# Attention and feed-forward block on one core: O transposed into SBUF and normalised one batch at a time

## The chip, the cores and the metric

The kernel runs on one core of one Trainium2 chip. The metric is the device time of one execution in microseconds. Engines are named as in the profile: PE (TensorE), PEld (its weight loads), DVE (VectorE), ACT (ScalarE), POOL (GpSimd), SP (SyncE, which issues all DMAs here).

## The reference, cut to what matters

For 16 batches of 256 tokens with 256 features in float32 (Python, shortened):

```
xn  = layernorm(x)                              # x: (16, 256, 256)
q, k, v = split(xn @ w_qkv)                     # 16 heads of 16
scores  = where(causal, (q / 4) @ k.T, -1e10)
o   = softmax(scores) @ v                       # per batch and head
out = x + o @ w_out + ffn(xn)                   # ffn: gated GELU in fp8, 256 -> 1024 -> 256
```

The output is (16, 256, 256) in float32.

## The kernel before, in words

The first third (to about 110 us) does the layernorm and the feed-forward part, adds its result to `xres` in SBUF, and stores the transposed, normalised tokens split into two fp32r parts. The rest is attention, one batch per step: the loop `for s in range(B)` in each engine's block (lines 1024, 564, 741, 374, 279), with B = 16. All order is written out by hand, an engine at a time; engines meet only at semaphores, and each engine takes its instructions strictly in order.

A batch b passes through several steps:

- `project_qk` and `project_v` (L845, L852, PE) make q, k and v; ACT copies and rounds them (L636, L642), POOL takes the low part (`split_qk`, L337), SP copies both parts into `stack` (`fill_stack`, three DMAs, L251).
- `max_scores(b, n)` for six units n = 0..5 (L905, PE) writes scores into three rotating banks of PSUM, and DVE's `find_max(b, n)` (L531) masks them and takes row maxima. `max_scores` of unit n waits (`max_done`, L898) until DVE has finished the first half of unit n - 1.
- `transpose_max(b, c)` (L963, PE) turns the maxima of half the heads (c = 0 or 1) once all their units are found; ACT negates them (L656), SP puts them into `stack` (`place_max`, L256).
- `exp_scores(b, n)` (L932, PE) waits for that DMA at n = 0 and 3, and for ACT's previous `exponent` (L663), since all units share two banks. ACT exponentiates into `arena`, POOL zeroes the masked half of diagonal blocks (`mask`, L366).
- `times_v(b, c)` (L954, PE, 32 passes) makes O for half the heads in one bank of PSUM (`pv_bank`), transposed and with the denominators as extra rows. Its next use of this bank waits for `o_norm_done` (L946).
- DVE: `o_to_rows(b, c)` (L540) transposes that bank in place in 32x32 blocks; `normalize_o(b, c)` takes the reciprocal of the denominators (L546), multiplies (L548, inputs: the bank in PSUM and `r_den` in SBUF; output `o_norm`), and transposes 128x256 into `ot_raw` (L555). ACT rounds it (`round_ot`, L672), POOL takes the low part (`split_ot`, L371), PE multiplies by w_out (`project_out`, L975), DVE adds `xres` (`add_x`, L561), SP stores it (L266).

In step s, PE works on maxima of batch s, exponentials of s - 1, O of s - 2 and s - 1, and the output of s - 3. In the order of time PE runs: `exp_scores(s-1, 0)`, `max_scores(s, 0)`, `transpose_max(s-1, 1)`, ..., `max_scores(s, 5)`, `times_v(s-1, 0)`. DVE runs `find_max(s-1, 5)`, `o_to_rows(s-2, 0)`, `find_max(s, 0..1)`, `normalize_o(s-2, 0)`, `find_max(s, 2)`, `o_to_rows(s-2, 1)`, `find_max(s, 3..4)`, `normalize_o(s-2, 1)`, `add_x(s-3)`. What comes after the loop (lines 1080 to 1101 of PE) ends the last two batches; `keep_warm(n, bank)` (L797) issues n transposes whose result nobody reads.

On SP, `fill_stack(s+1, 0)`, `load_xs(s+3)`, `store_y(s-4)` and `place_max(s, 0)` stand in this order in one queue. In the feed-forward part POOL waits for DVE's last normalisation of a chunk before it starts (line 343).

Of the kernel before, what the change touches and what calls it, by code (L numbers as in the profile page):

```python
# [31 lines left out]
def attention_ffn(nc, x, w_qkv, w_out, w_gating, w_linear, out):  # L32
# [25 lines left out]
    with ctx:  # L58
# [45 lines left out]
        r_den = sb("r_den", [P, H], F32)  # L104
# [1 line left out]
        o_norm = sb("o_norm", [P, S], F32)
        ot_part = xt_part[:, :, :, 0:S]
# [191 lines left out]
        def _(pool):  # L299
# [73 lines left out]

            for s in range(B):
                if has(s - 2):
                    mask(s - 2, 5)
                if has(s - 3):
                    split_ot(s - 3, 1)
# [10 lines left out]
                if has(s - 2):  # L389
                    split_ot(s - 2, 0)  # L390
# [13 lines left out]
        def _(dve):  # L404
# [136 lines left out]

            def normalize_o(b, c):
                done = 2 * b + c + 1
                o = pv_bank(b, c).rearrange("p (k e) -> p k e", e=2 * DH)
# [10 lines left out]
                nc.vector.transpose(ot_raw[:, c, :], o_norm[:, :]).then_inc(ot_ready, 1)  # L555

            def add_x(b):
# [3 lines left out]
                nc.vector.tensor_tensor(y[b % 2][:, :, :], misc[:, 0, :].rearrange("p (t d) -> p t d", t=QT),  # L561
                                        xres[:, b * QT:(b + 1) * QT, :], ALU.add).then_inc(y_done, 1)

            for s in range(B):
# [563 lines left out]
```

## Time and profile before

| | |
|---|---|
| median of 3 runs | 353.01 us (353.0 to 353.84) |
| profiled execution | 353.47 us, of it the span 351.8 us |
| busy over the span | PE 336.5 us (96%), DVE 294.5 (84%), ACT 227.2 (65%), POOL 167.8 (48%) |
| chain that ended last | PE 81%, DVE 10%, ACT 3%, issue 2%, DMA 2% |
| granted TensorE clock, mean | 0.995 |

The span runs from the first to the last instruction of the profiled execution, and all positions below are microseconds from its start. A group row gives busy time, then in brackets what the engine waited for before it. Matmul ends are modelled, so the start of the next PE group is the safer mark of when one was over. A step of attention takes 14.3 us: `exp_scores(s-1, 0)` starts at 291.17, 305.47 and 319.14 for s = 13, 14 and 15.

### The profile page before, as it was taken

Reading aid. Unit: us, or ns where it says so; the run is one execution under the profiler, and the core shown is the slowest. Engines: PE = TensorE matmul, PEld = TensorE weight load, DVE = VectorE, ACT = ScalarE, POOL = GpSimd, SP = SyncE. Lnnn points to the kernel's source line nnn. Section 1 sums busy time; section 2 is a strip of 40 time slices with the busy share of each in tenths; the row PEclk is TensorE's granted clock in tenths of the full one; section 3 lists DMA queues with packets and bytes.
Section 4 is the critical chain, followed back from the end, with each engine's and each line's share of the span. In section 5 each row is a group of like instructions: output and inputs, shape, how many; then the busy total and the mean of one; then the engine's idle time right before and its main releaser. Section 6 shows DMA issues by size and latency. Waiting matters only on the chain.

```text
span 351.8 us, 9794 instructions
## 1 busy us (share of the span) xinstructions
PE 336.5 (96%) x3514; PEld 256.8 (73%) x3514; DVE 294.5 (84%) x1359; ACT 227.2 (65%) x369; POOL 167.8 (48%) x203
## 2 busy tenths in 40 slices
PE   6899899999999999999999999999999999996996
PEld 6455456665676878788888888888888888884775
DVE  5897898888425787999999999899999999999865
ACT  1684777766655576676667766767667666775470
POOL 4214214422225364456675466664755657547461
PEclk9999999999999999999999999999999999999899
DMA  6959965673238243534528346274373552633011
GB/s 204 366 191 294 269 177 154 144 244 123 74 137 295 96 151 108 199 114 161 181 94 270 113 162 209 101 237 165 111 241 108 196 183 92 212 120 127 2 64 60
DMA packets 46569, 57.59 MB, mean 164 GB/s; under 512 B 2680, under 2 KB 39096, under 8 KB 46520
## 3 DMA queue, kind: packets, MB, share of 16 engines
q1 hardware_dynamic: 46520, 56.96, 49.9%
q8 instruction: 28, 0.46, 0.5%
q14 instruction: 21, 0.17, 0.2%
HBM read 16.78 MB, written 12.58 MB: 83 GB/s over the span
## 4 chain that ended last, share of the span: by engine, by line
PE 81%; DVE 10%; ACT 3%; issue 2%; DMA 2%; POOL 0%; SPq 0%; DVEq 0%; ACTq 0%; POOLq 0%
PE ps L954 13%; PE ps L845 13%; PE ps L932 11%; PE ps L905 9%; PE ps L852 7%; PE ps L832 7%; PE ps L975 6%; PE ps L809 6%; PE ps L815 6%; DVE masked L531 4%; PE ps L963 2%; PE ps L792 2%; ACT gate L618 1%; DMA xt_store<-stack 1%; DVE xn L432 1%
## 5 line engine op out<-in xcount | busy, mean ns | idle before, releaser
L531 DVE CUSTOM_DVE_ANT_0 masked<-ps,causal 128x256 bf16<-128x256 f32 (+1 forms) x512 | 148.2, 353 | 17.1 <-PE ps L905 17.1
L663 ACT ACTIVATE arena<-ps 128x1024 f32<-128x1024 f32 x96 | 98.1, 1026 | 54.7 <-PE ps L932 54.4
L366 POOL TENSOR_SCALAR_AFFINE_SELECT arena<-arena 128x512 f32<-128x512 f32 (+1 forms) x96 | 73.6, 787 | 32.9 <-ACT arena L663 32.9
L337 POOL TENSOR_TENSOR qk_part<-w_raw,qk_part 128x512 fp32r<-128x512 f32 x32 | 41.2, 1286 | 52.1 <-ACT qk_part L642 52.1
L618 ACT ACTIVATE gate<-ps 128x512 bf16<-128x512 f32 x64 | 38.6, 603 | 28.6 <-PE ps L809 28.3
L932 PE MATMUL ps<-stack 64*128 64x256 f32 (+1 forms) x512 | 51.4, 300 | 2.3 <-ACT arena L663 2.2
L845 PE MATMUL ps<-xs,wq_part 128*128 128x256 f32 x384 | 52.3, 285 | 0.3 <-ACT w_raw L636 0.3
L954 PE MATMUL ps<-arena,v_aug 128*32 128x256 f32 (+1 forms) x1024 | 49.5, 335 | 1.8 <-DVE o_norm L548 1.8
L905 PE MATMUL ps<-stack 63*128 63x256 f32 (+1 forms) x512 | 47.7, 285 | 2.0 <-DVE row_max L531 1.8
L845 PEld LDWEIGHTS ps<-xs,wq_part 128*128 128x128 f32 x384 | 47.5, 189 | 1.5 <-ACT w_raw L636 0.6
L932 PEld LDWEIGHTS ps<-stack 64*128 64x128 f32 x512 | 36.0, 186 | 15.0 <-issue 5.7
L531 DVE DVE_READ_ACCUMULATOR2_ANT row_max<- 128x1 f32 x512 | 42.6, 83 | 0.0
L954 PEld LDWEIGHTS ps<-arena,v_aug 128*32 128x32 f32 x1024 | 29.7, 111 | 17.4 <-issue 3.5
L905 PEld LDWEIGHTS ps<-stack 63*128 63x128 f32 x512 | 36.4, 187 | 6.4 <-DVE row_max L531 3.3
L333 POOL TENSOR_TENSOR xres<-xres,ffn 128x512 f32<-128x512 f32 x16 | 18.3, 1157 | 38.4 <-DVE xn L432 28.0
L468 DVE TENSOR_TENSOR arena<-ps,gate 128x512 fp8e4<-128x512 f32 x32 | 22.0, 687 | 15.7 <-ACT gate L618 15.3
L371 POOL TENSOR_TENSOR xt_part<-xn,xt_part 128x256 fp32r<-128x256 f32 x31 | 22.7, 731 | 20.0 <-ACT xt_part L672 20.0
L975 PE MATMUL ps<-wq_part,xt_part 128*128 128x256 f32 x192 | 30.7, 296 | 0.1
L540 DVE STREAM_TRANSPOSE ps<-ps 128x512 f32<-128x512 f32 x32 | 23.4, 731 | 5.3 <-PE ps L954 5.3
L468 DVE TENSOR_TENSOR act<-ps,gate 128x512 fp8e4<-128x512 f32 x32 | 21.8, 685 | 6.3 <-ACT gate L618 6.3
L852 PE MATMUL ps<-wq_part,xs 128*128 128x256 f32 x192 | 26.7, 288 | 0.0
L975 PEld LDWEIGHTS ps<-wq_part,xt_part 128*128 128x128 f32 x192 | 24.7, 189 | 2.8 <-issue 0.4
(64 smaller groups left out, 454.0 us busy)
## 6 DMA issues: line engine op xcount, KB each, us to landing
stack<-qk_part SPq DMA_DIRECT2D x96, 256.0 KB, 2.7
xs<-xt_store SPq DMA_DIRECT2D x16, 512.0 KB, 4.2
xt_store<-xt_part SPq DMA_DIRECT2D x14, 512.0 KB, 4.2
out_dram<-w_raw SPq DMA_DIRECT2D x15, 256.0 KB, 4.2
xres<-in_L_attn_x_dram SPq DMA_DIRECT2D x7, 512.0 KB, 6.6
arena<-in_L_ffn_w_gating_dram SPq DMA_DIRECT2D x2, 1024.0 KB, 9.3
stack<-zeros SPq DMA_DIRECT2D x4, 512.0 KB, 7.8
arena<-in_L_ffn_w_linear_dram SPq DMA_DIRECT2D x1, 1024.0 KB, 13.3
```

The lines of the kernel that those rows point to most:

```text
L337: nc.gpsimd.tensor_tensor(qk_part[:, g, QLO:KLO + 1:3, :], qk_raw[:, g, :, :], qk_part[:, g, QHI:KLO, :].bitcast(F32), ALU.subtract).then_ ...
L366: nc.gpsimd.affine_select(diag, diag, pattern=[[0, 1024 // width], [1, P]], compare_op=ALU.is_ge, fill=0.0, base=0, channel_multiplier=-1) ...
L468: nc.vector.tensor_tensor(act8[c % 2][:, j, :], up_ps[j % 2], gate[:, j % 2, :], ALU.mult, saturate=False).then_inc(act_done, 1)
L531: last = nc.vector.tensor_tensor_reduce(masked[:, place, i * width:(i + 1) * width], max_ps[:, place, i * width:(i + 1) * width], causal[: ...
L618: nc.scalar.activation(gate[:, j % 2, :], gate_ps[j % 2], ACT.Gelu_apprx_tanh).then_inc(gelu_done, 1)
L663: nc.scalar.activation(arena[:, n, :, :], exp_banks(b, n), ACT.Exp).then_inc(exp_done, 1)
L845: last = nc.tensor.matmul(misc[:, 1, s * S:(s + 1) * S], wq_part[:, a, kt, col:col + P], xs[b % 2][:, z, kt, :], start=(i == 0), stop=(i = ...
L852: last = nc.tensor.matmul(misc[:, 0, t * D:(t + 1) * D], xs[b % 2][:, z, kt, t * P:(t + 1) * P], wq_part[:, a, kt, 2 * D:3 * D], start=(i ...
L905: last = nc.tensor.matmul(max_ps[:, (2 * unit + u) % 3, i * width:(i + 1) * width], st[rows, j0 + i, 0, qt * P:(qt + 1) * P], st[rows, j0 ...
L932: last = nc.tensor.matmul(exp_banks(b, n)[:, u, i * width:(i + 1) * width], st[rows, j0 + i, 1, kt * P:(kt + 1) * P], st[rows, j0 + i, 0, ...
L954: last = nc.tensor.matmul(pv_bank(b, c)[32 * i:32 * i + 32, u * S + kt * P:(u + 1) * S], va[:, kt, 2 * (HG * c + i) + u, :], cols, start=( ...
L975: last = nc.tensor.matmul(y_bank(b, t), ot_part[:, z, c, t * P:(t + 1) * P], wq_part[:, a, c, 3 * D:4 * D], start=(first and i == 0), stop ...
```

## The change

1. `o_to_rows` transposes from PSUM into a new place `o_by_q[b % 2]` in SBUF (it reuses `wg8` and `act8[0]`, dead by then). `times_v` waits for `o_by_q_done` in place of `o_norm_done`.
2. `normalize_o` is called once a batch, on 32 denominators and 128x512 values, all of them in SBUF, for every batch but the last (`by_batch`). It stands where `normalize_o(s-2, 1)` stood. Likewise `round_ot` (ACT) and `split_ot` (POOL) are called once, 128x512, in the place of their former c = 1 calls. `ot_part` exists twice.
3. In step 15 and after it: DVE does `find_max(15, 5)` and `o_to_rows(14, 0)` before the normalisation of batch 13; `project_out(12, 1)` moves behind `times_v(14, 1)`; `project_out(13, 0)` behind `times_v(15, 0)`; `project_out(13, 1)` and both of batch 14 behind `times_v(15, 1)`; `keep_warm` is 8 in one place where it was 4 and 12 in two. Batch 14 gets the other bank of `misc` for its output.

The diff, without the bodies that only change an index:

```diff
             def o_to_rows(b, c):
 
                 dve.wait_ge(pv_ready, 2 * b + c + 1)
-                nc.vector.transpose(pv_bank(b, c), pv_bank(b, c)).then_inc(o_by_q_done, 1)
+                if b >= 2:
+
+                    dve.wait_ge(o_norm_done, 2 * b - 2)
+                nc.vector.transpose(o_by_q[b % 2][:, :, c, :], pv_bank(b, c).rearrange("p (u n) -> p u n", u=2)).then_inc(o_by_q_done, 1)
...
+                n = 2 if by_batch(b) else 1
+                half = slice(c, c + n)
+                done = 2 * b + c + n
+                o = o_by_q[b % 2][:, :, half, :].rearrange("p u c (k e) -> p u (c k) e", e=2 * DH)
+                den = r_den[:, :, half, :].rearrange("p u c k -> p u (c k)")
                 dve.wait_ge(o_by_q_done, done)
-                nc.vector.reciprocal(r_den[:, :], o[:, :, DH]).then_inc(den_done, 1)
+                nc.vector.reciprocal(den, o[:, :, :, DH]).then_inc(den_done, n)
...
+                nc.vector.tensor_tensor(o_norm[:, half, :].rearrange("p c (k u d) -> p u (c k) d", u=2, d=DH), o[:, :, :, 0:DH],
+                                        den.unsqueeze(3).broadcast_to([P, 2, n * S // 32, DH]), ALU.mult).then_inc(o_norm_done, n)
...
-                nc.scalar.copy(ot_part[:, 0, c, :], ot_raw[:, c, :]).then_inc(ot_hi, 1)
+                    act.wait_ge(ot_used, 2 * b + c + n - 4)
+                nc.scalar.copy(ot_part[b % 2][:, 0, half, :], ot_raw[:, half, :]).then_inc(ot_hi, n)
...
                 elif 2 * b + c >= 1:
-                    pe.wait_ge(o_norm_done, 2 * b + c)
+                    pe.wait_ge(o_by_q_done, 2 * b + c)
...
             exp_scores(B - 1, 0)
-            pe.wait_ge(y_done, B - 3)
-            project_out(B - 3, 0)
             pe.wait_ge(neg_done[0], B)
             transpose_max(B - 1, 1)
-            project_out(B - 3, 1)
             exp_scores(B - 1, 1)
             exp_scores(B - 1, 2)
             times_v(B - 2, 1)
+            project_out(B - 4, 1)
             for n in range(3, UNITS):
                 exp_scores(B - 1, n)
             times_v(B - 1, 0)
-            pe.wait_ge(y_done, B - 2)
-            project_out(B - 2, 0)
-
-            keep_warm(4, misc[:, 1, :])
+            pe.wait_ge(y_done, B - 3)
+            project_out(B - 3, 0)
             times_v(B - 1, 1)
-            project_out(B - 2, 1)
+            project_out(B - 3, 1)
+
+            pe.wait_ge(neg_done[1], B)
+            for c in range(2):
+                project_out(B - 2, c)
             pe.wait_ge(exp_done, UNITS * B)
             project_out(B - 1, 0)
-            keep_warm(12, misc[:, 1, :])
+            keep_warm(8, max_ps[:, 0, :])
             project_out(B - 1, 1)
```

On DVE, the end of step 14 before: after `find_max(14, 4)` the second half of batch 12 is normalised, then batch 11 gets `add_x`, then the maxima of unit 5 follow.

```order
L531 ISA masked,row_max<-ps,causal 128x256
L531 ISA row_max 128x1
L546 RECIPROCAL r_den<-ps 128x16 [waits o_by_q_done]
L548 TENSOR_TENSOR o_norm<-ps,r_den 128x2x8x16 [waits den_done]
L555 STREAM_TRANSPOSE xn<-o_norm 128x256 [waits ot_lo,o_norm_done]
L561 TENSOR_TENSOR w_raw<-ps,xres 128x512 [waits y_stored1,ot_used]
L531 ISA masked,row_max<-ps,causal 128x256 [waits max_ready]
```

The same place after the change:

```order
L537 ISA masked,row_max<-ps,causal 128x256
L537 ISA row_max 128x1
L559 RECIPROCAL r_den<-wg 128x32 [waits o_by_q_done]
L561 TENSOR_TENSOR xn<-wg,r_den 128x2x16x16 [waits den_done]
L566 STREAM_TRANSPOSE xn<-xn 128x512 [waits ot_lo,o_norm_done]
L573 TENSOR_TENSOR w_raw<-ps,xres 128x512 [waits y_stored1,ot_used]
L537 ISA masked,row_max<-ps,causal 128x256 [waits max_ready]
```

The three instructions of the normalisation became twice as long here, and the three in front of `find_max(s, 2)` are gone. The product reads `wg` (O) and `r_den`, both in SBUF, where it read `ps` and `r_den`.

On PE, the end before, from `times_v(15, 0)`'s last passes (L954) on:

```order
L954 MATMUL ps<-arena,v_aug 32x128 x4
L975 MATMUL ps<-wq_part,xt_part 128x256 [waits ot_lo,y_done]
L975 MATMUL ps<-wq_part,xt_part 128x256 x5
L797 MATMUL ps<-ident 128x128 x4
L954 MATMUL ps<-arena,v_aug 32x256 [waits o_norm_done,p_masked1]
```

and from `times_v(15, 1)`'s last passes on:

```order
L954 MATMUL ps<-arena,v_aug 32x128 x4
L975 MATMUL ps<-wq_part,xt_part 128x256 [waits ot_lo]
L975 MATMUL ps<-wq_part,xt_part 128x256 x5
L975 MATMUL ps<-wq_part,xt_part 128x256 [waits ot_lo,exp_done]
L975 MATMUL ps<-wq_part,xt_part 128x256 x5
L797 MATMUL ps<-ident 128x128 x12
L975 MATMUL ps<-wq_part,xt_part 128x256 [waits ot_lo_last]
L975 MATMUL ps<-wq_part,xt_part 128x256 x5
```

After the change, from `times_v(15, 1)`'s last passes on:

```order
L965 MATMUL ps<-arena,v_aug 32x128 x4
L986 MATMUL ps<-wq_part,xt_part 128x256 [waits ot_lo]
L986 MATMUL ps<-wq_part,xt_part 128x256 x5
L986 MATMUL ps<-wq_part,xt_part 128x256 [waits ot_lo,neg_done1]
L986 MATMUL ps<-wq_part,xt_part 128x256 x5
L986 MATMUL ps<-wq_part,xt_part 128x256 [waits ot_lo]
L986 MATMUL ps<-wq_part,xt_part 128x256 x5
L986 MATMUL ps<-wq_part,xt_part 128x256 [waits ot_lo,exp_done]
L986 MATMUL ps<-wq_part,xt_part 128x256 x5
L808 MATMUL ps<-ident 128x128 x8
L986 MATMUL ps<-wq_part,xt_part 128x256 [waits ot_lo_last]
L986 MATMUL ps<-wq_part,xt_part 128x256 x5
```

Behind the last `times_v` stand four groups of `project_out` ahead of the last one, where two stood, and eight transposes where twelve stood.

On POOL, the start of a step before: `mask(s-2, 5)`, `split_ot(s-3, 1)`, `split_qk(s+1, 0)`.

```order
L366 AFFINE_SELECT arena<-arena 128x4x128 [waits exp_done]
L371 TENSOR_TENSOR xt_part<-xn,xt_part 128x256 [waits ot_hi]
L337 TENSOR_TENSOR qk_part<-w_raw,qk_part 128x2x256 [waits qk_hi0]
```

and after:

```order
L373 AFFINE_SELECT arena<-arena 128x4x128 [waits exp_done]
L380 TENSOR_TENSOR xt_part<-xn,xt_part 128x2x256 [waits ot_hi]
L344 TENSOR_TENSOR qk_part<-w_raw,qk_part 128x2x256 [waits qk_hi0]
```

`split_ot` is twice as wide in this place and gone from its other one, behind `mask(s-1, 4)`.

## Rows read from the trace of the kernel before

**Rows 1.** Stretches: us, busy (count) by engine, clock, DMA share, GB/s.

```profile
280.00:300.00 20.00, 20.00 (x262) 16.64 (x259) 18.40 (x98) 14.17 (x22) 11.94 (x15) 1.00 0.40 134
```

**Rows 2.** Timeline of PE, start of step 14: start us, us, instruction group.

```profile
305.97 0.61 PE L905 MATMUL ps<-stack 63*128 63x128 f32 x8
306.51 0.38 PE L963 MATMUL ps<-ident,row_max 128*8 128x128 f32 x2
```

**Rows 3.** Timeline of ACT, POOL and DVE, end of step 13.

```profile
301.84 0.61 ACT L642 CAST qk_part<-w_raw 128x512 fp32r<-128x512 f32 x1
...
302.54 1.30 POOL L337 TENSOR_TENSOR qk_part<-w_raw,qk_part 128x512 fp32r<-128x512 f32 x1 [3.27 <-ACT qk_part L642]
...
302.54 0.25 DVE L546 RECIPROCAL r_den<-ps 128x16 f32<-128x16 f32 x1
302.83 0.42 DVE L548 TENSOR_TENSOR o_norm<-ps,r_den 128x256 f32<-128x256 f32 x1
303.29 0.45 DVE L555 STREAM_TRANSPOSE xn<-o_norm 128x256 f32<-128x256 f32 x1
...
303.66 0.65 DVE L561 TENSOR_TENSOR w_raw<-ps,xres 128x512 f32<-128x512 f32 x1
...
304.23 0.41 DVE L531 CUSTOM_DVE_ANT_0 masked<-ps,causal 128x256 bf16<-128x256 f32 x1
...
305.61 0.73 DVE L540 STREAM_TRANSPOSE ps<-ps 128x512 f32<-128x512 f32 x1
```

**Rows 4.** All L323 of POOL (ns min/median/max), and timeline at 13.8 us.

```profile
L323 POOL TENSOR_TENSOR rstd<-var_eps,minus_half x8: 1036/1037/1601, 5.9 to 80.7; 128x4 f32<-128x4 f32 x8
...
13.79 1.60 POOL L323 TENSOR_TENSOR rstd<-var_eps,minus_half 128x4 f32<-128x4 f32 x1
13.81 0.69 DVE L479 CAST wg<-arena 128x1024 fp8e4<-128x1024 f32 x1
```

**Rows 5.** Timeline of ACT, POOL and SP's queue, step 13.

```profile
295.63 0.40 ACT L672 CAST xt_part<-xn 128x256 fp32r<-128x256 f32 x1
...
296.11 0.73 POOL L371 TENSOR_TENSOR xt_part<-xn,xt_part 128x256 fp32r<-128x256 f32 x1 [1.47 <-ACT xt_part L672]
...
296.80 1.29 POOL L337 TENSOR_TENSOR qk_part<-w_raw,qk_part 128x512 fp32r<-128x512 f32 x1
...
298.12 1.87 SPq L251 DMA_DIRECT2D stack<-qk_part  x3
```

**Rows 6.** Timeline of PEld and SP's queue, starts of steps 5 and 8.

```profile
176.72 0.52 PEld L932 LDWEIGHTS ps<-stack 64*128 64x128 f32 x8 [0.23 <-DMA stack<-neg_max]
219.63 0.52 PEld L932 LDWEIGHTS ps<-stack 64*128 64x128 f32 x8 [0.20 <-DMA stack<-neg_max]
...
172.40 0.57 SPq L256 DMA_DIRECT2D stack<-neg_max  x1
...
216.19 0.57 SPq L256 DMA_DIRECT2D stack<-neg_max  x1
```

**Rows 7.** Timeline of PE from the end of step 14 on.

```profile
317.70 1.51 PE L954 MATMUL ps<-arena,v_aug 128*32 128x256 f32 x32 [0.65 <-DVE o_norm L548]
...
321.51 0.50 PE L905 MATMUL ps<-stack 63*128 63x256 f32 x4 [0.95 <-DVE row_max L531]
...
324.45 2.79 PE L954 MATMUL ps<-arena,v_aug 128*32 128x256 f32 x32 [0.35 <-DVE o_norm L548]
...
332.43 1.51 PE L954 MATMUL ps<-arena,v_aug 128*32 128x256 f32 x32 [0.65 <-DVE o_norm L548]
...
344.84 1.69 PE L975 MATMUL ps<-wq_part,xt_part 128*128 128x256 f32 x12
...
346.37 1.47 PE L797 MATMUL ps<-ident 128*128 128x128 f32 x12
...
347.90 0.97 PE L975 MATMUL ps<-wq_part,xt_part 128*128 128x256 f32 x6
```

**Rows 8.** The stretch of the lower clock, columns as in rows 1.

```profile
324.40:327.80 3.40, 3.35 (x40) 2.19 (x42) 2.25 (x10) 0.54 (x1) 1.24 (x3) 0.54 0.00 0
```

More of the change, by code:

```diff
@@ L103, in attention_ffn @@
         y = [w_raw[:, 0, i * QT * D:(i + 1) * QT * D].rearrange("p (t d) -> p t d", t=QT) for i in range(2)]
[L104 removed]
+        r_den = sb("r_den", [P, 2, 2, S // 32], F32)
+        o_by_q = [t.bitcast(F32).rearrange("p (u c n) -> p u c n", u=2, c=2)
+                  for t in (wg8[:, :, :, :].rearrange("p g k n -> p (g k n)"), act8[0][:, :, :].rearrange("p j t -> p (j t)"))]
         ot_raw = xn[:, 2:4, :]
[L106 to L107 removed]
+        o_norm = xn[:, 0:2, :]
+        ot_part = [xt_part[:, :, :, i * S:(i + 1) * S] for i in range(2)]
         ps = ctx.enter_context(nc.psum_tensor("ps", [P, 8, 512], F32))
@@ L161, in y_bank, with by_batch @@
         def y_bank(b, t):
-            return exp_ps[:, t, 0:D] if b == B - 1 else misc[:, 0, t * D:(t + 1) * D]
+            return exp_ps[:, t, 0:D] if b == B - 1 else misc[:, int(b == B - 2), t * D:(t + 1) * D]
+        def by_batch(b):
+            return b < B - 1
         block = ctx.enter_context(nc.Block())
@@ L377, in _ @@
                 if has(s - 3):
-                    split_ot(s - 3, 1)
+                    split_ot(s - 3, 0)
                 if s >= 1 and has(s + 1):
@@ L554, in normalize_o @@
                     dve.wait_ge(ot_lo, done - 2)
-                nc.vector.transpose(ot_raw[:, c, :], o_norm[:, :]).then_inc(ot_ready, 1)
+                nc.vector.transpose(ot_raw[:, half, :].rearrange("p c s -> p (c s)"),
+                                    o_norm[:, half, :].rearrange("p c s -> p (c s)")).then_inc(ot_ready, n)
             def add_x(b):
@@ L580, in _ @@
                     find_max(s, 4)
+                if s == B - 1:
+                    find_max(s, 5)
+                    o_to_rows(s - 1, 0)
                 if has(s - 2):
-                    normalize_o(s - 2, 1)
-                if has(s - 3):
+                    normalize_o(s - 2, 0)
+                if has(s - 3) and s < B - 1:
                     add_x(s - 3)
-            find_max(B - 1, 5)
-            o_to_rows(B - 2, 0)
+            o_to_rows(B - 2, 1)
+            add_x(B - 4)
             normalize_o(B - 2, 0)
-            add_x(B - 3)
-            o_to_rows(B - 2, 1)
-            normalize_o(B - 2, 1)
             for c in range(2):
@@ L745, in _ @@
                 if has(s - 3):
-                    round_ot(s - 3, 1)
+                    round_ot(s - 3, 0)
                 if has(s + 1):
@@ L756, in _ @@
                     negate_max(s, 0)
-                if has(s - 2):
-                    round_ot(s - 2, 0)
                 if has(s - 1):
@@ L770, in _ @@
                     round_qk(s + 2, 0)
-            round_ot(B - 3, 1)
             exponent(B - 1, 0)
@@ L776, in _ @@
             exponent(B - 1, 2)
-            round_ot(B - 2, 0)
+            round_ot(B - 3, 0)
             for n in range(3, UNITS):
                 exponent(B - 1, n)
-            round_ot(B - 2, 1)
+            round_ot(B - 2, 0)
             for c in range(2):
@@ L942, in times_v @@
                 if b == B - 1:
-                    pe.wait_ge(*((max_done, 2 * UNITS * B) if c == 0 else (o_norm_done, 2 * b)))
+                    pe.wait_ge(*((max_done, 2 * UNITS * B) if c == 0 else (o_by_q_done, 2 * b)))
                 elif 2 * b + c >= 1:
-                    pe.wait_ge(o_norm_done, 2 * b + c)
+                    pe.wait_ge(o_by_q_done, 2 * b + c)
                 for u in range(2):
@@ L1065, in _ @@
                     max_scores(s, 4)
-                if has(s - 3):
+                if has(s - 3) and s < B - 1:
                     project_out(s - 3, 1)
```

39 lines of the change are left out of this document (16 added, 23 removed).

## The prediction

> **What bounds the kernel now.** I read the stretches first. From 160 to 300 us PE has no idle time at all: 20.00 of 20 us, with DVE at 18.40, ACT at 14.17 and POOL at 11.94 [rows 1]. A step there takes as long as its PE instructions, so an edit on DVE, ACT or POOL can't shorten it; it can only put a wait into PE's row. So the question for each of the twelve full steps is a margin: how long before PE wanted it was each result ready. Then I read the timeline for the two places where a DVE result is nearly late. At the start of step 14 PE starts `max_scores(14, 0)` at 305.97, which needs the first half of `find_max(13, 5)`, and `transpose_max(13, 1)` at 306.51, which needs all of it [rows 2]. DVE starts that `find_max` at 304.23 and is through at 305.61, when its next instruction starts [rows 3]; half of it is then done at about 304.92. The margins are 1.05 and 0.90 us, less about 0.1 for the semaphore. Last I read the end, from step 14 on, where PE does wait: 0.65 us ahead of 317.70, 0.95 ahead of 321.51, 0.35 ahead of 324.45 and 0.65 ahead of 332.43; the three of `times_v` are for `o_norm_done` [rows 7]. One `times_v` there takes 2.79 us where the others take 1.51, and the clock granted between 324.4 and 327.8 is 0.54, so for most of it the lower level, 1.2 GHz [rows 7, 8]. The idle stretches come just ahead of it.
>
> **The waits for o_norm_done.** They go, since the bank is free after one transpose. In the full steps PE never waited there, so that is worth nothing. At the end it can be worth up to 0.65 + 0.35 + 0.65 = 1.65 us, if nothing else is late next.
>
> **The merged normalisation on DVE.** Per batch one set of three instructions goes and the other doubles. The product grows by 0.23 us (0.65 of a 128x512 TENSOR_TENSOR less 0.42 of the 128x256 one), the transpose by 0.28 (0.73 less 0.45), the reciprocal by some 0.02 [rows 3]. DVE gains in sum: a set took 302.54 to 303.66, 1.12 us, and the growth is 0.53, so 0.6 us a step less work. But the gain lies ahead of `find_max(s, 2)`, where DVE waits for PE anyway, and the growth lies ahead of `find_max(s, 5)`. That one moves from 304.23 to 304.76. Of the margins 1.05 and 0.90 remain 0.52 and 0.37, less 0.1. Price in the full steps: nothing, but the cover is then 0.3 us thin.
>
> **What the product now reads.** Before, L548 read O from PSUM and the denominators from SBUF. Now both inputs lie in SBUF. It would start at about 302.85, and POOL has been in `split_qk` since 302.54 and stays until 303.84 [rows 3]; POOL's start hangs on ACT's rounding (L642, 301.84), which follows PE, so the two meet like this in every full step. Does one of the two block the other? No row shows a DVE instruction with two SBUF inputs beside a POOL one. The nearest row: L323 on POOL takes 1.04 us in seven of eight places and 1.60 where it started within 0.02 us of a DVE copy from SBUF to SBUF (L479, 0.69 us). POOL lost 0.56 of 0.69 us, four fifths of what the other took; DVE lost nothing, the copy ran like its peers [rows 4]. So a blocking exists between these engines, and it is nearly whole. In the new place POOL is first by 0.3 us, so DVE should be the one that loses. Bounds: 0, and 0.98 us (302.85 to 303.84). I take four fifths of the upper one, 0.8 us, by rows 4. Then all maxima are found at 305.61 + 0.53 + 0.8 = 306.94, PE sees it at 307.04 and not at 306.51: 0.53 us in each step. By the upper bound it is 0.71. The step repeats rigidly from PE to PE, so the loss isn't made up: it comes at the start of steps 3 to 14, twelve times, 6.4 us (0 to 8.5).
>
> The Trainium skill's page "SBUF — State Buffer", section "Who interferes with whom", says that a DVE instruction with two SBUF inputs contends with a GpSimd instruction that reads SBUF, that whichever starts first holds the shared pair for its whole instruction, and that a DVE instruction with at most one SBUF input does not contend. By that the sum would take the upper end. The trace agrees as far as it goes: L548 and L555, one SBUF input each, keep their 0.42 and 0.45 us beside POOL's 1.30 [rows 3]; two inputs no run has shown yet.
>
> **POOL and ACT ahead of fill_stack.** ACT's `round_ot` grows from 0.40 to 0.61 us (L642 has the new width, rows 3), POOL's `split_ot` from 0.73 to 1.29 (as L337). POOL stands idle for `round_ot` here (1.47 us), and `split_qk(s+1, 0)` and SP's `fill_stack(s+1, 0)` follow without a gap [rows 5]. So this train of DMAs starts 0.21 + 0.56 = 0.77 us later, and behind it in SP's queue stand `load_xs`, `store_y` and `place_max(s, 0)`, which `exp_scores(s, 0)` waits for. The place of that DMA shows a thin margin: in step 5 it was issued at 172.40 and let PE go at 176.72, 4.3 us later; in step 8, issued late at 216.19, it did so at 219.63, 3.4 us later [rows 6]. With 3.4 us an ordinary issue has 0.9 us to spare and 0.77 costs nothing; with 4.3 it costs all of it. Two of the ten full steps name the DMA, so I take 2 x 0.77 = 1.5 us (0 to 8 x 0.77 = 6). If the product blocks as above, PE waits for DVE in the same half microsecond afterwards and a stall at `exp_scores` is largely contained in it, so then I count nothing more.
>
> **The end.** The first wait, 0.65 ahead of 317.70, goes, but `find_max(14, 5)` comes 0.53 later and with it everything of DVE up to the 0.95 us wait ahead of 321.51: PE gets there at 322.04, later than before. `times_v(13, 1)` loses its 0.35 and starts at about 324.6, 0.2 late. PE has idled as much before it, so I keep its 2.79 us. After that PE saves 0.65 at 332.43 and several groups of `project_out` move back; what binds is ACT's exponentials, and I get `times_v(15, 1)` ending 1.1 us earlier than 344.84. Behind it come four groups of six passes where two took 344.84 to 346.37, 0.77 each, and 8 transposes where 12 took 1.53 [rows 7]: + 1.53 - 0.51 = + 1.0. The remainder, rounding, low part and last product, is the same. Net 0.1 us gain or loss, taken as + 0.1 for the store of batch 13 that now falls near the end. A blocked product in step 14 adds its 0.8 at 321.51 once more, on a chain of DVE, PE and ACT that has no slack.
>
> **Sum.** 353.5 (profiled execution) + 6.4 + 0.8 + 0.1 = 360.8. The profiled execution is 0.46 above the median of 353.01, so against the medians 360.3 us.
>
> **Rivals.**
> 1. No blocking, but the DMA train is late: 353.0 + 1.5 + 0.1 = 354.6. For it: [rows 5, 6]; against it: eight of ten steps don't name the DMA. It decides where `place_max` lands less than 0.77 us before `exp_scores`.
> 2. Nothing new binds: 353.0 + 0.1 = 353.1. For it: DVE has less work, 0.3 us of cover is left. It needs both the product and the train to be hidden.
> 3. The other side, faster: no blocking, and PE keeps its full clock in step 15. The place is `times_v(13, 1)`: 1.51 in place of 2.79 us, 1.3 less, and the 0.2 it starts late is then swallowed by ACT. 353.1 - 1.4 = 351.7. For it: two waits of PE shortly before are removed or moved, and a clock that fell once beside 0.95 and 0.35 us waits may not fall with others. Against it: the wait for maxima ahead of 321.51 grows. It decides from the point where PE's idle time between 318 and 324 is less than before.
>
> The change surely does what it says on DVE; a variant of the forecast is a partial blocking, 0.3 to 0.5 us on the product, which costs 0.03 to 0.2 a step and ends between 353.5 and 356.
>
> **How the numbers follow.** A measurement of this kernel tells no change from one within about 0.3%, 1.06 us. Forecast (blocking) 0.47; rival 1 0.15; rival 2 0.16; rival 3 0.22. Faster by over 0.3% is rival 3, 0.22; within it rival 2 and a little of rival 1, 0.17; slower the rest, 0.61. The forecast's own range is 356 (partial) to 363.5 (the upper bound, 0.71 in twelve steps and 0.98 at the end: 353.0 + 8.5 + 1.0 + 0.1 = 362.6, and some for DMAs). The range for 8 in 10 must reach rival 3: 351.4 to 363.
>
> **What would show it.** The product (now L561) at about 1.2 to 1.6 us, or started that much late, where 0.65 is its free size; a period from `exp_scores` to `exp_scores` of 14.8 to 15.0 us where it was 14.3; PE waiting for `row_max` ahead of `transpose_max` in each step. If the product takes 0.65 to 0.70 beside `split_qk`, the forecast is wrong. If PE waits for `neg_max`'s DMA, it is rival 1; if no L954 is over 1.6 us long, rival 3.

## The result, and the profile after

| | before | changed kernel |
|---|---|---|
| median, taken together | 353.42 us (4 runs) | 368.49 us (366.15 to 369.75, 4 runs) |
| profiled execution, span | 353.47, 351.8 us | 368.86, 367.1 us |
| granted TensorE clock, mean | 0.995 | 0.981 |

The ratio is 1.0384 [1.0332, 1.0435], 15.1 us slower. The direction and the mechanism in the steps were as forecast; the size was twice the forecast's 7.3 us, and the time lies outside the range.

From the page of the changed kernel: busy time, the granted clock in 40 slices, and the chain that ended last. PE's share fell from 96% to 93% although it did 6 us more of busy time, and DVE's share of the chain rose from 10% to 23%.

```profile
PE 342.4 (93%) x3506; PEld 259.1 (71%) x3506; DVE 297.1 (81%) x1314; ACT 225.2 (61%) x354; POOL 171.7 (47%) x188
...
PEclk9999999999999999999999999999999999996599
...
PE 52%; DVE 23%; DMA 8%; issue 6%; ACT 4%; SPq 4%; POOL 2%; DVEq 0%; ACTq 0%; POOLq 0%
```

The timeline of DVE, POOL and PE where step 13 ends (start us, us, engine, line; what was waited for in brackets) answers to [rows 2, 3]:

```profile
296.56 0.35 DVE L559 RECIPROCAL r_den<-wg 128x32 f32<-128x32 f32 x1
296.56 1.29 POOL L344 TENSOR_TENSOR qk_part<-w_raw,qk_part 128x512 fp32r<-128x512 f32 x1 [2.44 <-ACT qk_part L654]
297.01 1.38 DVE L561 TENSOR_TENSOR xn<-wg,r_den 128x512 f32<-128x512 f32 x1
...
297.80 2.14 POOL L373 TENSOR_SCALAR_AFFINE_SELECT arena<-arena 128x1024 f32<-128x1024 f32 x2
...
298.49 0.71 DVE L566 STREAM_TRANSPOSE xn<-xn 128x512 f32<-128x512 f32 x1
...
299.12 0.65 DVE L573 TENSOR_TENSOR w_raw<-ps,xres 128x512 f32<-128x512 f32 x1
299.70 0.41 DVE L537 CUSTOM_DVE_ANT_0 masked<-ps,causal 128x256 bf16<-128x256 f32 x1
299.80 0.52 PEld L943 LDWEIGHTS ps<-stack 64*128 64x128 f32 x8 [0.50 <-DMA stack<-neg_max]
...
300.61 0.66 PE L916 MATMUL ps<-stack 63*128 63x128 f32 x8
...
301.07 0.71 DVE L549 STREAM_TRANSPOSE act<-ps 128x512 f32<-128x512 f32 x1
```

The product takes 1.38 us. Its record begins at 297.01, in the middle of POOL's `split_qk` (296.56 to 297.85), and ends at 298.39, 0.54 us behind POOL's end: a blocked instruction shows here as a long one, not as a late one. POOL loses as well: the two masks behind `split_qk`, which start beside the product, take 2.14 us, where the kernel without the overlap (e1 below) shows 1.68. From the reciprocal to `find_max(13, 5)` are 299.70 - 296.56 = 3.14 us, where it was 304.23 - 302.54 = 1.69 [rows 3].

All that PE and its loads waited for in the steps, 148 to 326 us (total us, times, longest):

```profile
PE ps L943 <- DMA stack<-neg_max: 2.7, 6, 1.3
PE ps L916 <- DVE row_max L537: 2.7, 8, 0.5
...
PEld ps L943 <- DMA stack<-neg_max: 5.3, 9, 1.6
```

Both suspects of the prediction show, DVE's maxima and the DMA behind the late train. A step that ran at 14.3 us takes 15.07, from one `transpose_max(s-1, 1)` on PE to the next:

```profile
301.30 0.38 PE L974 MATMUL ps<-ident,row_max 128*8 128x128 f32 x2
...
316.37 0.38 PE L974 MATMUL ps<-ident,row_max 128*8 128x128 f32 x2
```

The stretches of PE at the end (us, busy, granted clock, DMA share, GB/s), which answer to [rows 1, 8]:

```profile
300.00:320.00 20.00, 19.34 (x228) 1.00 0.35 121
...
330.00:340.00 10.00, 7.12 (x72) 0.68 0.23 79
340.00:350.00 10.00, 8.50 (x80) 0.64 0.00 1
...
333.60:347.30 13.70, 11.94 (x104) 0.50 0.06 20
```

The clock is at its lower level, 1.2 GHz, for 13.7 us, where it was 3.4 us before [rows 8]. PE's own timeline there answers to [rows 7]:

```profile
330.76 0.66 PE L916 MATMUL ps<-stack 63*128 63x128 f32 x8 [1.81 <-DVE row_max L537]
...
332.81 0.50 PE L916 MATMUL ps<-stack 63*128 63x256 f32 x4 [0.98 <-DVE row_max L537]
...
334.66 0.80 PE L943 MATMUL ps<-stack 64*128 64x256 f32 x4 [1.11 <-ACT arena L675]
...
335.82 2.79 PE L965 MATMUL ps<-arena,v_aug 128*32 128x256 f32 x32
...
345.30 2.46 PE L965 MATMUL ps<-arena,v_aug 128*32 128x256 f32 x32
```

Three waits of 1.81, 0.98 and 1.11 us stand around the fall. Before they were 0.95 and 0.35 [rows 7] and, between these two, 1.12, which this row of the kernel before shows:

```profile
323.37 0.50 PE L932 MATMUL ps<-stack 64*128 64x256 f32 x4 [1.12 <-ACT arena L663]
```

Two `times_v` are slow instead of one. Last, the kernel's final adds on DVE:

```profile
364.02 0.76 DVE L613 TENSOR_TENSOR w_raw<-ps,xres 128x256 f32<-128x256 f32 x2 [1.75 <-DMA out_dram<-w_raw]
```

The add waits 1.75 us, with the store of batch 13 named as releaser; before it waited 0.78 us for the last matmuls.

### The profile page after: what moved, and what is told of

The parts are those of the page before. It is cut to its first block, busy times and chain, and to the rows that moved or that the text cites. A ratio compares the mean times of both kernels' runs of the same rounds, so it can differ in the third digit from the quotient of the medians.

```text
span 367.1 us, 9748 instructions
## 1 busy us (share of the span) xinstructions
PE 342.4 (93%) x3506; PEld 259.1 (71%) x3506; DVE 297.1 (81%) x1314; ACT 225.2 (61%) x354; POOL 171.7 (47%) x188
## 4 chain that ended last, share of the span: by engine, by line
PE 52%; DVE 23%; DMA 8%; issue 6%; ACT 4%; SPq 4%; POOL 2%; DVEq 0%; ACTq 0%; POOLq 0%
DVE masked L537 10%; PE ps L856 8%; PE ps L916 8%; PE ps L965 6%; PE ps L943 6%; PE ps L863 6%; PE ps L843 5%; PE ps L820 5%; PE ps L826 5%; DVE xn L561 4%; DMA stack<-neg_max 3%; DMA xres<-in_L_attn_x_dram 2%; SPq L258 2%; PE ps L974 2%; DVE w_raw L573 1%
## 5 line engine op out<-in xcount | busy, mean ns | idle before, releaser
L373 POOL TENSOR_SCALAR_AFFINE_SELECT arena<-arena 128x512 f32<-128x512 f32 (+1 forms) x96 | 79.8, 852 | 41.2 <-ACT arena L675 41.1
L943 PE MATMUL ps<-stack 64*128 64x256 f32 (+1 forms) x512 | 52.5, 306 | 6.7 <-ACT arena L675 3.8
L916 PE MATMUL ps<-stack 63*128 63x256 f32 (+1 forms) x512 | 49.4, 292 | 6.7 <-DVE row_max L537 6.3
L943 PEld LDWEIGHTS ps<-stack 64*128 64x128 f32 x512 | 36.8, 191 | 20.4 <-ACT arena L675 5.5
L965 PE MATMUL ps<-arena,v_aug 128*32 128x256 f32 (+1 forms) x1024 | 50.5, 340 | 0.0
L916 PEld LDWEIGHTS ps<-stack 63*128 63x128 f32 x512 | 37.8, 192 | 12.5 <-issue 6.0
L380 POOL TENSOR_TENSOR xt_part<-xn,xt_part 128x512 fp32r<-128x512 f32 (+1 forms) x16 | 20.1, 1255 | 32.1 <-ACT xt_part L686 32.1
L863 PEld LDWEIGHTS ps<-wq_part,xs 128*128 128x128 f32 x192 | 23.5, 188 | 2.0
## 6 DMA issues: line engine op xcount, KB each, us to landing
arena<-in_L_ffn_w_linear_dram SPq DMA_DIRECT2D x1, 1024.0 KB, 13.7
```

Of the source, the lines that this page charges most:

```text
L373: nc.gpsimd.affine_select(diag, diag, pattern=[[0, 1024 // width], [1, P]], compare_op=ALU.is_ge, fill=0.0, base=0, channel_multiplier=-1) ...
L863: last = nc.tensor.matmul(misc[:, 0, t * D:(t + 1) * D], xs[b % 2][:, z, kt, t * P:(t + 1) * P], wq_part[:, a, kt, 2 * D:3 * D], start=(i ...
L916: last = nc.tensor.matmul(max_ps[:, (2 * unit + u) % 3, i * width:(i + 1) * width], st[rows, j0 + i, 0, qt * P:(qt + 1) * P], st[rows, j0 ...
L943: last = nc.tensor.matmul(exp_banks(b, n)[:, u, i * width:(i + 1) * width], st[rows, j0 + i, 1, kt * P:(kt + 1) * P], st[rows, j0 + i, 0, ...
L965: last = nc.tensor.matmul(pv_bank(b, c)[32 * i:32 * i + 32, u * S + kt * P:(u + 1) * S], va[:, kt, 2 * (HG * c + i) + u, :], cols, start=( ...
```

## The experiments

Each kernel's median is compared with that of the kernel before from the same chip. "Growth" is by how much `transpose_max(14, 0)` of the profiled execution came later than in the kernel before (313.65 us there), less the same for `transpose_max(2, 0)` (142.57 there): the loss of twelve steps alone. "Low clock" is the length of the stretch at 1.2 GHz ahead of PE's last products, again in the profiled execution. "Product" is the duration of the multiplication in `normalize_o` (us); where two are given, they are the first and the second half of a batch.

| kernel | product | growth | low clock | median, us | ratio [95%] |
|---|---|---|---|---|---|
| before | 0.42 | 0 | 3.4 | 353.4 to 353.6 | 1 |
| changed kernel | 1.38 | 9.6 | 13.7 | 368.49 | 1.0384 [1.0332, 1.0435] |
| e1_guard | 0.69 | 5.7 | 6.8 | 359.89 | 1.0168 [1.0118, 1.0218] |
| e2_swap | 1.38 | 9.0 | 6.8 | 366.78 | 1.0371 [1.0303, 1.0438] |
| e3_both | 0.69 | 1.1 | 13.7 | 359.94 | 1.014 [1.0064, 1.0215] |
| e4_halves | 0.98, 1.27 | 2.2 | 6.8 | 359.79 | 1.0169 [1.0115, 1.0223] |
| e5_sbuf_old_end | 0.98, 1.27 | 1.7 | 3.4 | 356.62 | 1.0099 [1.0065, 1.0132] |
| e6_guard_old_end | 0.42 | -0.3 | 6.8 | 354.44 | 1.0029 [1.0001, 1.0057] |
| e7_before_warm | 0.42 | 0.0 | none | 352.44 | 0.9968 [0.995, 0.9986] |
| e8_guard_warm | 0.42 | -0.3 | none | 351.80 | 0.9946 [0.9921, 0.9972] |
| e9_after_warm | 1.38 | 9.6 | none | 363.18 | 1.0273 [1.0243, 1.0304] |
| e10_both_warm | 0.69 | 1.0 | none | 353.88 | 1.0015 [0.9995, 1.0035] |
| e11_both_warm_y3 | 0.69 | 1.0 | none | 353.45 | 1.0007 [0.9985, 1.0029] |

**e1_guard: POOL waits until the product is done.** This adds nothing to DVE; it moves `split_qk(s+1, 1)` behind the product, so that the two never overlap.

```diff
 if s >= 1 and has(s + 1):
+    if has(s - 2):
+        pool.wait_ge(o_norm_done, 2 * (s - 2) + 2)
     split_qk(s + 1, 1)
```

> The changed kernel, but in each step from 2 on POOL's split_qk(s+1, 1) waits until DVE has finished the product of batch s-2, so that the two never run together. Theory 1 (the product with two SBUF inputs is blocked by POOL, and this is what makes PE late): the product takes 0.65 to 0.70 us where it took 1.38, find_max(s, 5) starts 0.7 us earlier, PE no longer waits for row_max in the full steps. Theory 2 (the DMA train behind fill_stack is late as well, by the wider split_ot): PE still waits for the neg_max DMA at the start of most steps. If theory 1 alone holds the time is 358 to 360 us (368.5 less twelve times 0.76). If the train binds by itself, 362 to 366. Rival (the product is slow by its own access pattern, not by POOL): it stays at 1.38 and the time at 368 or more.

Measured: 359.89 us. The product (L563 here; min/median/max in ns) is at its free size, and the masks of POOL behind it are short again:

```profile
L563 DVE TENSOR_TENSOR xn<-act,r_den x6: 692/693/693, 160.4 to 308.9; 128x512 f32<-128x512 f32 x6
...
295.99 1.68 POOL L373 TENSOR_SCALAR_AFFINE_SELECT arena<-arena 128x1024 f32<-128x1024 f32 x2
...
PE ps L945 <- DMA stack<-neg_max: 4.6, 6, 1.4
PEld ps L945 <- DMA stack<-neg_max: 7.1, 9, 1.7
```

The last two rows are all of the waits for other engines that the view lists for PE and its loads from 148 to 312 us. So with the blocking gone PE shows no wait for DVE, and of the 5.7 us of growth that remain, 4.6 are PE's six waits for the DMA behind the late train; e3_both shows what the other 1.1 are. The time lies where blocking alone was expected (358 to 360), and yet the train binds as well: that expectation priced a blocked product and nothing beside it.

**e2_swap: the train early again.** On POOL, `split_qk(s+1, 0)`, which the train waits for, goes ahead of the now longer `split_ot`.

```diff
-if has(s - 3):
-    split_ot(s - 3, 0)
 if s >= 1 and has(s + 1):
     split_qk(s + 1, 0)
+if has(s - 3):
+    split_ot(s - 3, 0)
```

> The changed kernel, but in each step POOL does split_qk(s+1, 0) ahead of split_ot(s-3), so that the three DMAs of fill_stack, and place_max behind them in the queue, start earlier than in the kernel before. Theory 1 (the blocked product alone sets the loss): PE waits for no neg_max DMA any more, but as long for row_max, and the time stays at 366 to 369 us. Theory 2 (the late DMA train sets it): the time falls to 359 to 362.

Measured: 366.78 us. The product stays at 1.38, and in the same stretch the only wait of PE is

```profile
PE ps L916 <- DVE row_max L537: 5.0, 11, 0.5
```

Eleven times, once a step. With the train early the growth is still 9.0 us, nearly that of the whole change. The two causes overlap, they don't add: 5.7 and 9.0 us with one of them, 9.6 with both, and 1.1 of each of these is what e3_both has with neither.

**e3_both: both edits.**

> Both edits at once: POOL's split_qk(s+1, 1) waits for the product, and split_qk(s+1, 0) goes ahead of split_ot(s-3). By both theories nothing else in the full steps is late: a step takes 14.3 us again, PE idles nowhere from 160 to 300 us, and the time is 357 to 359.5 us: what is then left above the kernel before, 4 to 6 us, is the end (lower clock for 13.7 us, four groups of project_out behind the last times_v, the last store). If the step stays above 14.5 us, a third cause is at work.

Measured: 359.94 us (355.79 to 360.26). The view lists no wait of PE for another engine between 148 and 312 us, and the growth is 1.1: blocked product and late train are all of the loss in the steps but this 1.1. The timeline shows what it is:

```profile
304.27 0.35 DVE L561 RECIPROCAL r_den<-act 128x32 f32<-128x32 f32 x1
...
306.72 0.41 DVE L539 CUSTOM_DVE_ANT_0 masked<-ps,causal 128x256 bf16<-128x256 f32 x1
...
307.71 0.61 PE L918 MATMUL ps<-stack 63*128 63x128 f32 x8
308.09 0.71 DVE L551 STREAM_TRANSPOSE wg<-ps 128x512 f32<-128x512 f32 x1
308.32 0.38 PE L976 MATMUL ps<-ident,row_max 128*8 128x128 f32 x2
```

From the reciprocal to `find_max(13, 5)` are 306.72 - 304.27 = 2.45 us, 0.76 more than the 1.69 before, with nothing blocked. The maxima are found at 308.09 and PE goes on 0.23 us later, as in the changed kernel (301.07 and 301.30); it is 0.22 to 0.24 us at this place in every full step of this kernel, where it was 0.87 us or more before. So of the 0.90 us of margin [rows 2, 3] only 0.67 can be used, and 0.76 - 0.67 = 0.09 us a step are lost, in waits too short for the view. Twelve times that is the 1.1. The merged normalisation costs this by its own length.

A step takes 14.4 us, as expected, and the time is 0.4 above its range (357 to 359.5). It is still 6 us slower than before, and now nearly all of that comes after 320 us. Its stretches (columns as above) show the clock:

```profile
320.00:330.00 10.00, 6.74 (x80) 0.77 0.31 107
330.00:340.00 10.00, 9.31 (x82) 0.55 0.00 1
```

**e4_halves: the changed kernel with its end, normalised half a batch at a time.** `by_batch` returns False, and the calls of `normalize_o`, `round_ot` and `split_ot` stand in the loop's old places. O stays in SBUF.

```diff
 def by_batch(b):
-    return b < B - 1
+    return False
```

> The changed kernel with O in SBUF as there, but normalised, rounded and split by halves, each half in the place where the kernel before had it; the order of the end is the changed one. It separates the two SBUF inputs from the merging. Theory 1: the half product ahead of find_max(s, 5) meets split_qk as well and takes 0.42 + 0.8 = 1.2 us; of the 0.90 us margin some 0.7 are usable, so 0.2 us a step are lost, 2.4 us in all, and no DMA is late; with the 5 us of the end 360 to 362 us. Rival (the merging itself costs, blocking is minor): the same 358 to 360. Rival (two SBUF inputs are slow in any form): every half product takes over 0.8 us, those too that no POOL instruction meets.

Measured: 359.79 us. The half products are blocked too. The first row has all of those that read one of the two buffers (min/median/max in ns: the first of a batch takes 0.98 us, the second 1.27), the others show a second one and POOL beside it:

```profile
L564 DVE TENSOR_TENSOR xn<-act,r_den x12: 982/1122/1275, 153.3 to 305.2; 128x256 f32<-128x256 f32 x12
...
290.41 1.28 POOL L344 TENSOR_TENSOR qk_part<-w_raw,qk_part 128x512 fp32r<-128x512 f32 x1 [3.09 <-ACT qk_part L660]
...
290.71 1.26 DVE L564 TENSOR_TENSOR xn<-wg,r_den 128x256 f32<-128x256 f32 x1
```

The product ends at 291.97, 0.28 us after POOL's 291.69. The first half product meets POOL's `split_ot`, and `split_qk` behind that takes 1.47 us instead of 1.28:

```profile
283.98 0.73 POOL L380 TENSOR_TENSOR xt_part<-xn,xt_part 128x256 fp32r<-128x256 f32 x1 [1.63 <-ACT xt_part L692]
284.01 0.99 DVE L564 TENSOR_TENSOR xn<-wg,r_den 128x256 f32<-128x256 f32 x1
```

It ends at 285.00, 0.29 us behind POOL's 284.71. Behind step 15, where no POOL instruction meets it, a half product takes 0.42 us (349.06 to 349.48), so two inputs in SBUF aren't slow by themselves. A growth of 2.2 us follows, 0.18 a step: with halves, some 0.5 us less stands ahead of `find_max(s, 5)` and the train isn't late, so blocking of the same kind costs a quarter. Again some 4 us are lost at the end. The time is 0.2 below the range of the expectation it bears out (360 to 362) and inside that of its rival (358 to 360), so it is the rows that decide between the two.

**e5_sbuf_old_end: the kernel before, O in SBUF, nothing else.** Halves, and before's end.

```diff
-nc.vector.transpose(pv_bank(b, c), pv_bank(b, c)).then_inc(o_by_q_done, 1)
+nc.vector.transpose(o_by_q[b % 2][:, c, :], pv_bank(b, c)).then_inc(o_by_q_done, 1)
...
-o = pv_bank(b, c).rearrange("p (k e) -> p k e", e=2 * DH)
+o = o_by_q[b % 2][:, c, :].rearrange("p (k e) -> p k e", e=2 * DH)
...
-pe.wait_ge(o_norm_done, 2 * b + c)
+pe.wait_ge(o_by_q_done, 2 * b + c)
```

> The kernel before with only this changed: O is transposed into SBUF (two places), times_v waits for that transpose; normalisation by halves, and everything in the order of before, the end too. Against e4_halves it differs in the order of the end alone. Theory (blocking of the half products): as in e4 each full step loses 0.2 us, 2.2 in all, and the second half product takes 1.25 us; the waits of times_v for o_norm_done at the end are gone, worth 0 to 1.6 us. So 354 to 355.7 us, and the new order of the end is what makes e4 4 to 5 us slower than this. Rival (the order of the end costs nothing and the low clock is a matter of the idle time that any of these have there): 358 to 360, as e4.

Measured: 356.62 us, above what was expected (354 to 355.7). Against e4_halves the end differs, and the layout of O in SBUF and the second `ot_part`: 3.2 us between the medians, of which 0.5 is growth in the steps (2.2 against 1.7). In the profiled executions the low clock lasts 3.4 against 6.8 us, which is at most 1.7 of it.

**e6_guard_old_end: e5_sbuf_old_end with both waits on POOL.** `split_qk(s+1, 0)` first, then `split_ot(s-3, 1)` behind a wait for the first product, and e1's wait.

```diff
+if has(s - 2):
+    pool.wait_ge(o_norm_done, 2 * (s - 2) + 1)
 if has(s - 3):
     split_ot(s - 3, 1)
```

> e5_sbuf_old_end, but POOL never reads SBUF while a half product runs: split_qk(s+1, 0) goes ahead of split_ot(s-3, 1), which waits for the first half product, and split_qk(s+1, 1) waits for the second. Theory: all half products take 0.40 to 0.43 us, a step takes 14.31 us, and of the waits at the end up to 1.6 us is saved: 352 to 353.4. Rival (at the end ACT and DVE are late next, so that the removed waits come back elsewhere): the same as before, 353.0 to 353.9.

Measured: 354.44 us, a miss for both. The products are back at 0.42 us, and the twelve steps are 0.3 us shorter in all than before's, but the stretch at the lower clock is twice as long as before (the row answers to [rows 8]):

```profile
L554 DVE TENSOR_TENSOR o_norm<-act,r_den x12: 424/425/547, 153.3 to 303.1; 128x256 f32<-128x256 f32 x12
...
320.00:330.00 10.00, 7.87 (x81) 0.66 0.32 107
```

**e7_before_warm: the kernel before with 15 transposes in step 15.** Two idle places of PE are filled with `keep_warm`, whose result nobody reads.

```diff
 transpose_max(s - 1, 1)
+if s == B - 1:
+    keep_warm(7, misc[:, 1, S:2 * S])
...
 exp_scores(s - 1, 1)
+if s == B - 1:
+    keep_warm(8, misc[:, 1, S:2 * S])
```

> The kernel before, with 7 transposes that nobody reads put ahead of max_scores(15, 1) and 8 ahead of exp_scores(14, 2), in the two gaps of PE (0.95 and 1.12 us) just ahead of the stretch in which the clock fell. If that fall hangs on PE's idle time shortly before, it doesn't come or is shorter, and times_v(13, 1) takes 1.5 us in place of 2.8: 351.7 to 352.3. If it doesn't, or if the transposes hold up what follows, 353 to 354.5.

Measured: 352.44 us, 0.1 above the range given for the case that the fall hangs on these idle places (351.7 to 352.3), and below that for the other case (353 to 354.5). `times_v(13, 1)` takes 1.51 us again [rows 7], and waits of PE that stay are as short as 0.19 and 0.34:

```profile
320.92 0.93 PE L797 MATMUL ps<-ident 128*128 128x128 f32 x7
322.03 0.50 PE L905 MATMUL ps<-stack 63*128 63x256 f32 x4 [0.19 <-DVE row_max L531]
...
322.70 1.09 PE L797 MATMUL ps<-ident 128*128 128x128 f32 x8
...
324.98 1.51 PE L954 MATMUL ps<-arena,v_aug 128*32 128x256 f32 x32 [0.34 <-DVE o_norm L548]
```

**e8_guard_warm: e6_guard_old_end with the same transposes.**

> e6_guard_old_end with the 15 transposes of e7_before_warm. If both effects hold they add up: 350.5 to 352. If only one holds, 352 to 353.4. If the gaps have moved so that the transposes stand in the way, over 353.5.

Measured: 351.80 us, ratio 0.9946 [0.9921, 0.9972], the lowest median of all kernels here, where both effects together were expected (350.5 to 352). The 2.6 us from e6_guard_old_end to this one are the clock. The 0.64 from e7_before_warm to this one would be what the earlier release of PSUM is worth once the product is not blocked, but the runs of the two overlap (351.79 to 353.41 against 351.19 to 353.51), so a gain is likely and not shown.

**e9_after_warm: the changed kernel, PE kept busy in step 15.** 14 transposes behind `exp_scores(14, 0)`, and e7's 7 and 8.

```diff
+if s == B - 1:
+    keep_warm(14, misc[:, 1, S:2 * S])
 if has(s):
     max_scores(s, 0)
```

> The changed kernel with 29 transposes of the identity put into TensorE's three idle places of step 15 (14 behind exp_scores(14,0), 7 behind transpose_max(14,1), 8 behind exp_scores(14,1)), and nothing else. Theory (the granted clock is what the end lost): the stretch at half clock, 333.64 to 347.29 in the profiled run of the changed kernel, held some 11.8 us of matmuls, which take 5.9 us less at the full clock; in the kernel before the same trick gave 0.65 of such a sum, so 3.8 to 5.9 us: 362.6 to 364.7 us, clock 0.998 or more. Rival (the end's length comes from its waits and from the project_out groups behind times_v(15,1), and the clock only falls beside them): 367.5 to 369 us with the clock at full.

Measured: 363.18 us, 5.3 less than the changed kernel and within the range for the clock (362.6 to 364.7). The stretches show the full clock throughout:

```profile
330.00:340.00 10.00, 9.53 (x116) 1.00 0.28 97
340.00:350.00 10.00, 7.48 (x114) 1.00 0.05 18
```

**e10_both_warm: e3_both with the same 29 transposes.**

> e3_both (POOL's copies neither before nor behind the product) with the same 29 transposes. Theory (clock): e3_both's 359.9 less 3.8 to 5.9, so 354.0 to 356.1 us; what is then left over the kernel before is the 0.9 us of the steps, the wait of the last add for the store of batch 13 and what the new order of the end itself costs. Rival (waits and order): 359 to 360.5 us.

Measured: 353.88 us, 6.1 less than e3_both and 0.1 below the theory's lower end; ratio to the kernel before 1.0015 [0.9995, 1.0035], so no difference that can be measured.

```profile
320.00:330.00 10.00, 9.76 (x119) 1.00 0.32 107
330.00:340.00 10.00, 7.63 (x116) 1.00 0.08 27
...
348.72 0.76 DVE L615 TENSOR_TENSOR w_raw<-ps,xres 128x256 f32<-128x256 f32 x2 [1.31 <-DMA out_dram<-w_raw]
```

**e11_both_warm_y3: e10_both_warm, the last add into a third buffer.**

```diff
-dve.wait_ge(y_stored[1], 16 * (B // 2 - 1))
...
-nc.vector.tensor_tensor(y[1][:, t, :], y_bank(B - 1, t), ...)
+nc.vector.tensor_tensor(y_end[:, t, :], y_bank(B - 1, t), ...)
```

> e10_both_warm with the last two adds of the residual written into a third buffer, so that they do not wait until the store of batch 13 has read the second one. Theory (the store on the path: the last add of e3_both began 1.31 us late with DMA as releaser, the matmuls it also needs having ended some 1 us before): 0.9 to 1.3 us below e10_both_warm. Rival (the add would wait for the last matmuls in its place): within 0.3 us of e10_both_warm.

Measured: 353.45 us, 0.4 below e10_both_warm. The wait for the store is gone, and the one for the last matmuls takes half of its place:

```profile
348.35 0.78 DVE L615 TENSOR_TENSOR w_raw<-ps,xres 128x256 f32<-128x256 f32 x2 [0.60 <-PE ps L988]
```

1.31 - 0.60 = 0.7 us by the trace, 0.4 by the medians, whose intervals overlap. Neither expectation was met; the store costs something between 0 and 0.7 us.

## Why the prediction was wrong

The sum to explain is 15.1 us against 7.3 predicted. The kernels with the full clock split it. The fall costs the changed kernel 5.3 us (e9_after_warm) and the kernel before 1.1 (e7_before_warm), so 4.2 net. Blocking and late train, in the steps and in step 15, cost 363.18 - 353.88 = 9.3 (e9_after_warm, e10_both_warm). What is left, 353.88 - 352.44 = 1.4 (e10_both_warm, e7_before_warm), is 1.0 of growth in the steps, the merged normalisation's own length (e3_both), and 0.4 at the end. That makes 14.9. The prediction had 0 for the clock, 6.4 + 0.8 = 7.2 for blocking and train, 0 for the length and 0.1 for the end. So the clock is over half of what was missing.

**The failed step is the one on the end: "PE has idled as much before it, so I keep its 2.79 us".** It priced the lower clock at what it had cost before. The waits were even predicted well: "a blocked product in step 14 adds its 0.8 at 321.51 once more", and in the trace the wait that stood at 321.51 [rows 7] ends at 332.81, 11.3 us later where the steps had lost 9.9; 1.4 more, with 0.53 + 0.8 = 1.33 predicted. But those idle places were counted once, as waits, and the clock stayed down for 13.7 us behind them and not for 3.4. In e9_after_warm they are filled and nothing else is changed: the clock stays up, and 5.3 us come back where the kernel before gets back 1.1. That the fall hangs on the idle places is shown by this; what sets its length is not.

**The blocking was right, and its price was too low.** Bounds of 0 and 0.98 us were given, and 0.8 taken from [rows 4]. Measured is 1.38 - 0.69 = 0.69, a little less than the 0.84 that POOL still had (297.85 less 297.01): behind POOL's end the product ran for 0.54 us, 0.15 less than its free 0.69. As a step it is well sized, though [rows 4], from which the price came, shows another pairing: a DVE copy with one input in SBUF, beside which it was POOL that lost. What was too small is what stands around it. The normalisation grew by 3.14 - 1.69 = 1.45 us where the prediction had 0.53 + 0.8 = 1.33: 0.69 by the blocking and 0.76, not 0.53, by its own length (e3_both). The reciprocal of 32 takes 0.35 and not 0.27. PE followed DVE by 0.23 us, not by the assumed 0.1: maxima found at 301.07, transposed at 301.30. By the prediction's own sum that gives 1.45 + 0.23 - 0.90 = 0.78 us a step; measured is 0.75 (9.0 us in 12 steps, e2_swap), predicted was 0.53. For the same two reasons "price in the full steps: nothing" for the merged normalisation was wrong: 0.76 + 0.23 - 0.90 = 0.09 a step, 1.1 in all. The Trainium skill, "SBUF — State Buffer", "Who interferes with whom", says that the one that starts first holds the shared pair for its whole instruction; by the upper bound the prediction had 0.71 a step, 8.5 us, and the trace agrees with that end: the product ends a fixed time after POOL's instruction.

**The late train was priced too low, and it did not matter beside the blocking.** Predicted alone, 1.5 us (bounds 0 and 6); measured alone, 4.6, which is 5.7 (e1_guard) less the 1.1 of e3_both and also the sum of PE's waits for that DMA. These are six waits of 0.77 us on average. The price of one step was right, and the error was to take the number of steps whose row named the DMA, two, as the number of steps without slack. That the stall would be "largely contained" in the other one was right: both together are 9.6, 0.6 more than with the train early (e2_swap).

**The order of the end.** Predicted + 0.1, with 0.1 in it for the store of batch 13; measured + 0.4 at the full clock, of which that store is all or none (0 to 0.7 us, e11_both_warm_y3). A small error.

**The rivals.** None held alone; the late train of rival 1 is there, beside the blocking. Rival 3 asked the right question, whether the clock falls, and put its point of decision at the idle time between 318 and 324, but only looked at the side where idle time shrinks. The other side, a longer fall, was what happened, and no case priced it. Of what was to be seen, the product of 1.2 to 1.6 us, PE waiting for `row_max` and a longer period came; the period is 15.07 us, just above the 14.8 to 15.0.

**What stays open.** What sets the length of the fall. e1_guard, e2_swap and e3_both have the same last two waits (0.98 and 1.12 us) ahead of it, and e1_guard and e3_both the same 1.13 before those, yet it lasts 6.8, 6.8 and 13.7 us. The changed kernel and e2_swap also share the wait before those, 1.81 us, and have 13.7 and 6.8. One run of e3_both took 355.79 us at a mean clock of 0.988 where the others took 360 at 0.981, so it varies within a kernel. It does so in the kernel before too: of its 57 runs beside the experiments, the six with a mean clock of 0.985 took 355.28 to 355.79 us, the eight with 0.998 or more 352.0 to 353.71. With a fall that long in some runs and short in others, a single profile doesn't tell two versions of this end apart.

## What to carry to other kernels

When an edit moves an operand from PSUM to SBUF, look for every POOL instruction beside its reader: here a DVE product with two SBUF inputs and POOL's instructions excluded each other, and the one that came second paid the rest of the other's instruction, which falls on the path if DVE feeds PE. When a margin is to hide something, take from it the time from DVE's end to PE's start as a row shows it, 0.23 us here. Where PE's clock has already dipped once, price each new idle place near it twice, as a wait and as half speed for what follows; a few matmuls whose result nobody reads, put into such a place, took the second price away in all five kernels that had them. And before you call a transfer hidden, ask how much slack it has in the steps that don't name it.

## What the runs showed of the hardware

- A blocked instruction shows its wait as duration. The product of 128x512 ended 0.54 us behind POOL's (298.39 against 297.85), those of 128x256 0.28 and 0.29 us behind (291.97 against 291.69, 285.00 against 284.71), though one had lost 0.84 and the other 0.57. POOL is blocked the same way: two masks that start beside the product take 2.14 us for 1.68, and a `split_qk` of e4_halves takes 1.47 for 1.28. The Trainium skill, "SBUF — State Buffer", "Who interferes with whom", has the rule, and the trace agrees in both directions.
- A product with one input in PSUM ran beside POOL's 1.30 us at 0.42 us [rows 3]; from SBUF, with POOL idle, it takes 0.42 us as well (e6_guard_old_end). The place of the operand costs nothing by itself.
- From the end of DVE's maxima, taken as the start of its next instruction, to PE's transpose of them were 0.22 to 0.24 us in every full step of e2_swap and e3_both, where PE waited for them (e3_both: 308.09 to 308.32).
- Stretches at 1.2 GHz of 3.4, 6.8 and 13.7 us came with waits of PE of 0.35 to 1.81 us each, while PE was busy for 11.94 of 13.70 us in the longest. With those places filled, the mean clock was 0.998 or more in every run of five kernels.
